# An expert weight's norm product two tiles later, and a reordered first down half, in a one-core attention and mixture-of-experts kernel

## The reference

```python
x = x + tanh(g_xattn) * xattn(layernorm(x), ctx, w_xattn)      # x: 16 x 128 x 1024
x = x + tanh(g_ffn) * ffn(layernorm(x), ...)

def xattn(feature, embedding, weight):   # three taps of the row, each weighted by a cosine of neighbours
    sim = stack([cos(emb, emb_left), cos(emb, emb), cos(emb, emb_right)])
    return einsum('bit,oi->bot', unfold3(feature) * repeat(sim, C), weight)

def ffn(h):
    rw = top2(h @ gate_w).sum(-1)
    shared = relu(h @ up_w) ** 2 @ down_w                  # 1024 -> 2048 -> 1024
    routed = ((h @ fc1_w) @ expert_w * rw) @ fc2_w         # 1024 -> 512 -> 512 -> 1024
    return layernorm(shared + routed, ln_gamma, ln_beta)
```

## Time and profile before

| what | value |
|---|---|
| median of 3 runs | 993.27 us |
| profiled execution | 992.8 us, span from first to last instruction 990.8 us |
| TensorE busy | 945.3 us, 95% of the span |
| VectorE, ScalarE, GpSimd busy | 491.2 us, 323.3 us, 319.0 us |
| mean granted TensorE clock | 0.985 of 2.4 GHz |
| TensorE's waits | 13.3 us (first weights), 10.6 us (L1309), 6.6 us (L1411), 2.7 us (L1357) |

### The profile page before, as it was taken

The page is one execution under the profiler, slowest core; times in us unless marked ns, Lnnn a source line. Parts: engine busy times, 40 slices in busy tenths (PEclk is TensorE's granted clock), DMA queues, the critical chain, the costliest instruction groups (busy, mean ns, idle before and its releaser), DMA issues.

```text
span 990.8 us, 12369 instructions
## 1 busy us (share of the span) xinstructions
PE 945.3 (95%) x4562; PEld 441.1 (45%) x4562; DVE 491.2 (50%) x859; ACT 323.3 (33%) x437; POOL 319.0 (32%) x147
## 2 busy tenths in 40 slices
PE   4989599799999999999999999999999999999995
PEld 2448244344444444444444444444444444444442
DVE  6677678985762345365662236355563222211112
ACT  3578775743331123242321122233332122211111
POOL 4220322238572431242572422142672200001110
PEclk9999799889999999999999999999999999999998
DMA  8796976343414543323414443422324233200001
GB/s 318 258 350 234 358 277 216 87 128 86 125 46 128 177 150 131 109 86 86 127 43 129 163 144 130 130 86 85 100 71 128 86 107 107 64 1 21 9 14 43
DMA packets 63359, 127.15 MB, mean 128 GB/s; under 512 B 35250, under 2 KB 35378, under 8 KB 62146
## 3 DMA queue, kind: packets, MB, share of 16 engines
q1 hardware_dynamic: 62290, 124.04, 38.2%
q10 hardware_dynamic: 1008, 2.30, 0.8%
HBM read 100.96 MB, written 19.07 MB: 121 GB/s over the span
## 4 chain that ended last, share of the span: by engine, by line
PE 85%; DVE 4%; ACT 3%; DMA 2%; issue 2%; DVEq 1%; ACTq 1%; SPq 1%; POOL 0%
PE psS L1411 32%; PE psS L1357 20%; PE psR L1357 20%; PE psR L1421 8%; PE psP L1320 5%; DMA big<-in_w_fc 1%; DVEq L906 1%; DMA xT<-in_ctx 1%; ACT hid L801 1%; DVE s L935 0%; ACT hid L812 0%; DVE ring L971 0%; DMA sim_scratch<-simo 0%; ACTq L811 0%; DVE s L939 0%
## 5 line engine op out<-in xcount | busy, mean ns | idle before, releaser
L1411 PE MATMUL psS<-big,hid 128*128 128x512 f16 x1536 | 337.4, 381 | 6.9 <-issue 6.6
L1411 PEld LDWEIGHTS psS<-big,hid 128*128 128x128 f16 x1536 | 150.4, 98 | 189.2 <-issue 9.4
L1357 PE MATMUL psS<-xT,ring 128*128 128x512 f16 (+1 forms) x912 | 191.5, 370 | 3.8 <-DVE xT L1060 2.7
L1357 PE MATMUL psR<-xT,ring 128*128 128x512 f16 (+1 forms) x912 | 190.2, 368 | 0.0
L1357 PEld LDWEIGHTS psS<-xT,ring 128*128 128x128 f16 x912 | 89.9, 99 | 102.5 <-DVE xT L1060 2.8
L1357 PEld LDWEIGHTS psR<-xT,ring 128*128 128x128 f16 x912 | 89.3, 98 | 97.1
L542 POOL TENSOR_TENSOR y<-y,lgb 128x1024 f32<-128x1024 f32 x15 | 39.2, 2612 | 252.8 <-ACT y L679 252.8
L1078 DVE SCALAR_TENSOR_TENSOR y<-psR,rw,y 128x1024 f32<-128x1024 f32 x15 | 19.2, 1281 | 141.0 <-PE psR L1421 141.0
L1421 PE MATMUL psR<-w,lgb 128*128 128x512 f16 x384 | 85.5, 379 | 0.0
L512 POOL TENSOR_TENSOR sides<-scr 128x1024 f32<-128x1024 f32 x12 | 30.1, 2506 | 141.7 <-DMA scr<-in_ctx 141.7
L532 POOL TENSOR_TENSOR ring<-f_buf,ring 128x1024 f32<-128x1024 f32 x18 | 39.2, 2177 | 99.7 <-ACT f_buf L647 60.4
(11 more groups left out here) (203 smaller groups left out, 989.1 us busy)
## 6 DMA issues: line engine op xcount, KB each, us to landing
ring<-pair_scratch SPq DMA_DIRECT2D x60, 512.0 KB, 3.3
ring<-sim_scratch SPq DMA_DIRECT2D x18, 504.0 KB
big<-in_w_up SPq DMA_DIRECT2D x8, 1024.0 KB, 6.4
out_rows<-y SPq DMA_DIRECT2D x15, 512.0 KB, 3.0
hid<-in_w_down SPq DMA_DIRECT2D x14, 512.0 KB, 6.1
big<-in_w_down SPq DMA_DIRECT2D x14, 512.0 KB, 6.9
pair_scratch<-ring SPq DMA_DIRECT2D x12, 512.0 KB, 6.9
scr<-in_ctx SPq DMA_DIRECT2D x9, 576.0 KB, 3.8
```

Source lines behind the costliest of these rows:

```text
L1357: mm = pe.matmul(up_bank[t % NR][:, cols], rows[:, a, k, :], xT[:, k, b, cols], start=(k == 0 and a == 0 and b == 0), stop=(k == KB - 1 an ...
L1411: mm = pe.matmul(psS[:, HALF * h:HALF * h + HALF], hT[:, i, a, P * j:P * j + P], dn[:, i, b, HALF * h:HALF * h + HALF], start=(i == 0 and ...
```

## The change

Five edits, all in the start-up stage and in block 0:

- `W2_SCALE_T` goes from 5 to 7: TensorE's small product for `w2` stands behind tile 6 instead of tile 4, and VectorE's reading of it at t = 7 instead of 5.
- The first row of down half 0: TensorE makes the whole shared product, then the routed one, then the attention of row (1, 0); before, that attention stood behind 12 of 16 slices.
- The same shared product waits for each slice of its input (`h_rdy`, i+1) and of the weights; before, it waited ahead of its first matmul for 14 of the 16 input slices and for `w2`. The wait for `w2` now stands ahead of the routed product.
- ScalarE and VectorE follow: the last three slices of the down matrix are split ahead of the rounding of row (1, 0) and of the routing, and the taking of row 0's result (`take_s`, `take_r`, `y_stats`, `finish`) comes ahead of `combine`. `take_s` now waits for `f_los` and `f_lo` of row (1, 0), as it writes a buffer that these read.
- In the start-up stage the turned halves of row 1 are taken out of PSUM earlier: on ScalarE ahead of `w2_evac(3)` and one square of the up matrix, on VectorE ahead of `combine(0, 2)`.

```diff
-        W2_SUM_T, W2_SCALE_T = 3, 5
+        W2_SUM_T, W2_SCALE_T = 3, 7
-        XATTN_AT, XATTN_FIRST = (5, 0, 0, 0), (12, 12, 10, 6)
+        XATTN_AT, XATTN_FIRST = (5, 0, 0, 0), (None, 12, 10, 6)
@@ ScalarE, end of up half 0
+                    for c in DN_LATE:
+                        dn_split_hi(c)
                 if phase_a:
                     f_his(m, 0)
@@ ScalarE, down half
                     if first and j == 0:
-                        for c in DN_LATE:
-                            dn_split_hi(c)
+                        act.wait_ge(f_lo_v, 2)
+                        act.wait_ge(f_lo_p, 1)
+                        take_s(n, j, phase_a)
                     if phase_a:
                         if j < BB - 1:
                             std(LX, BB * m + j + 1)
                             f_rows(m, j + 1)
+                        if first and j == 0:
+                            finish(n, j)
                         std(L1, BB * m + j)
                         x1_normal(m, j)
                         x_hi(m, j)
-                        if first and j == 0:
-                            take_s(n, j, phase_a)
                         if j < BB - 1:
                             f_his(m, j + 1)
@@ ScalarE, start-up
             up_square(0)
-            up_square(1)
-            w2_evac(3)
             first_xt_hi(1, 0)
             first_xt_hi(1, 1)
+            w2_evac(3)
+            up_square(1)
@@ VectorE, end of up half 0
+                if first:
+                    for c in DN_LATE:
+                        dn_lo(c)
+                    f_los(m, 0)
                 routing(n)
-                if phase_a:
+                if phase_a and not first:
                     f_los(m, 0)
@@ VectorE, down half
-                    if first and j == 0:
-                        for c in DN_LATE:
-                            dn_lo(c)
                     if phase_a:
                         if j < BB - 1:
                             x_stats(m, j + 1)
+                        if first and j == 0:
+                            take_r(n, j)
+                            y_stats(n, j)
                         combine(m, j)
                         x_lo(m, j)
@@ VectorE, start-up
-            combine(0, 2)
             first_xt_lo(1, 0)
             first_xt_lo(1, 1)
+            combine(0, 2)
             combine(0, 3)
@@ TensorE, shared()
                     if first:
+                        pe.wait_ge(h_rdy, i + 1)
                         pe.wait_ge(dn_rdy, i + 1)
@@ TensorE, down half
+                    if first and j == 0:
+                        pe.wait_ge(up_evac, UT - 2)
+                        shared(0, 0, IT, True).then_inc(s_done, 1)
+                        pe.wait_ge(up_evac, UT)
+                        pe.wait_ge(w2_rdy, LT)
+                        routed(0, 0, LT).then_inc(r_done, 1)
+                        xattn(m, 0)
+                        continue
                     if j == 0:
                         pe.wait_ge(up_evac, UT * (n + 1) - 2)
                         pe.wait_ge(h_rdy, IT * (n + 1) - 2)
-                        if first:
-                            pe.wait_ge(w2_rdy, LT)
```

More of the change, by code:

```diff
@@ L776, in down_half @@
                         take_s(n, j, phase_a)
-                    if phase_a or j < BB - 1:
-                        finish(n, j)
+                        if phase_a or j < BB - 1:
+                            finish(n, j)
                 if not phase_a:
@@ L1214, in down_half @@
                         continue
-                    take_r(n, j)
-                    y_stats(n, j)
+                    if not (first and j == 0):
+                        take_r(n, j)
+                        y_stats(n, j)
             def last_rows():
@@ L1440, in down_half @@
                         done = (XATTN_FIRST if first else XATTN_AT)[j]
-                        shared(j, 0, done, first and j == 0)
+                        shared(j, 0, done)
                         xattn(m, j)
                     if j == 0:
-                        shared(j, done, IT - 2, first)
+                        shared(j, done, IT - 2)
                         done = IT - 2
                         pe.wait_ge(h_rdy, IT * (n + 1))
-                    shared(j, done, IT, first and j == 0).then_inc(s_done, 1)
+                    shared(j, done, IT).then_inc(s_done, 1)
                     if j > 0:
```

## The result

The changed kernel takes **1003.5 us** (median of 4 runs, 1002.39 to 1006.71), the kernel before 992.7 us in the same comparison (four runs, 991.49 to 993.35). The ratio is 1.0119, 95% interval 1.0098 to 1.014: slower by 1.2% (the two medians lie 10.8 us apart), where 990.2 us had been forecast. The profiled execution took 1002.39 us with a span of 1000.6; the one before 992.8 with 990.8.

The account below looks back on a forecast made before the run. TensorE is busiest (945.3 of 990.8 us), but other engines keep most of its 24 us at stake. Up half 2.4 plus row 2's start 0.9 less loads 0.2 gives 3.1 us: median 990.2 us, range 984.5 to 994.5.

Parts of the forecast that it names:

- the start of row 2: First down half: psS free at 257.9 us instead of 260.98, 3.1 us gained, or 0.9 us after the slow clock.
- the 0.2 taken off for the loads: Row (1, 3): later cosine loads move `f_lo` to 296 or 297.5 us, close to TensorE's need at 297.65; 0.2 us lost.
- The up half, 2.4 us: Start-up and first up half: 1.1 us from the earlier turned halves and 1.3 us from the `w2` edit.
- the prediction's own sign ("or not at all"): Tile 19's relu at 197.5 us (before 199.94); forecast wrong if over 4 us earlier or not earlier at all.
- the give-back: Up half: `w2`'s scale takes 1.6 us of VectorE's lead; tile 8's lo half meets GpSimd, ending about 1.9 us late.
- this meeting: End of up half, 195.81 us: VectorE's lo half waited for GpSimd, taking 2.83 us instead of 0.68.
- The slow clock: Half clock on TensorE behind the 5.9 us stall ahead of row 2, costing 2.2 us.
- The rigid chain: GpSimd, first down half: `weigh` of row (1, 2) starts 16.0 us behind `f_lo` of row (1, 1).
- the first down half's start without a wait: First shared product: TensorE starts at 192.0 us, gaining the whole 6.62 us wait and the slow clock there.
- The small product behind tile 14: Up half, down matrix: a new TensorE wait of 5 to 8 us (there at 150.8, sum ready about 158), costing nothing.
- The slower one: Rival 3: row (1, 3)'s late cosine loads stop TensorE a second time, 995.4 us; chance 0.12.

Follow-up runs that it names:

- e5: The changed kernel with GpSimd finishing row (0, 0) ahead of `weigh` of row (1, 2): 996.85 us, ratio 1.0055 to the kernel before.
- e6: The changed kernel with both e4's spread additions and e5's earlier finish of row (0, 0) on GpSimd: 992.63 us, ratio 1.0021 to the kernel before.
- e11: The changed kernel with e9's order of GpSimd: 994.17 us, ratio 1.0026 to the kernel before.
- e3: The kernel before with the down half edits alone, without the `w2` and start-up edits: 1001.06 us, ratio 1.0106.
- e8: The kernel before with only the first shared product's waits changed (input rows one by one, `w2` ahead of the routed product): 991.64 us, ratio 1.0004.
- e9: e8 with GpSimd's first down half reordered: three additions later, rows (0, 0) and (0, 1) finished ahead of `weigh`: 990.29 us, ratio 0.999 to the kernel before.
- e10: e9 with the first attention behind 14 slices instead of 12 and `take_s` of row (0, 0) earlier: 987.93 us, ratio 0.9962 to the kernel before.
- e12: The kernel before with e9's order of GpSimd alone: 991.5 us, ratio 1.0003.
- e4: The changed kernel with GpSimd's additions of the first down half spread, three of four moved behind later rows' `f_lo`: 999.36 us, ratio 1.008 to the kernel before.
- e7: e6 with ScalarE's `take_s` of row (0, 1) ahead of the three roundings of row (1, 2): 997.0 us, ratio 1.0051 to the kernel before.
- e1: The kernel before with the `w2` edit alone (small product behind tile 6, read at t = 7): 990.87 us, ratio 0.9998.
- e2: The kernel before with the start-up edit alone (row 1's turned halves taken earlier): 992.24 us, ratio 1.0011.

## Why the prediction was wrong

The forecast was 990.2 us, the measured time 1003.5: outside the range, and on the other side.

- **The step that failed** is in the first down half: "ScalarE rounds the third row, 1.0 us, and only then comes `take_s` of row (0, 1), 1.1 us: psS is free at 257.9 us." GpSimd and the roundings came as reckoned on the clock of before, without the 2.4 us that were to come off: `f_lo` of row (1, 1) at 232.5 (233.2), `weigh` 16.1 us behind it at 248.55 (249.2), the third rounding done at 257.3 (256.8). But `take_s` waits also for the store of row (0, 0), which stands behind `weigh` and the finish on GpSimd: 265.6 + 1.1 = 266.7. In the prediction's sum the start of row 2 counted as 3.1 us gained, with 2.4 more from the up half; it was 5.8 us lost. e5, e6 and e11 show it: with the finish ahead of `weigh` the wait falls to 10.9, 6.0 and 6.9 us and the ratio from 1.0119 to 1.0055, 1.0021 and 1.0026, which is 6.3, 9.7 and 9.2 us.
- **The numbers for it were there.** The store of before went out 4.9 us behind the end of `weigh` (251.92 to 256.80) and landed 2.7 us later. Behind the forecast's own `weigh`, done at 255.8, that is an estimate of 263.4 us for the landing and 264.5 for psS, 3.5 us after today's start and not 3.1 before. The other 2.2 us are GpSimd's longer instructions, less its start of 0.7 us ahead of the forecast.
- **The sum.** The forecast span was 987.7 us, the measured one 1000.6. The 12.9 us between them are 11.3 at the start of row 2 (5.8 lost, 5.5 forecast as gained), 0.3 of slow clock, 1.5 at the loop's second pass, which the forecast had at nothing, less the 0.2 taken off for the loads.
- The prediction read `take_s`'s releaser from the rows of before, where two came together and only the rounding shows. The code has the second in the line above the copy (`act.wait_ge(out_done, ...)`). It follows GpSimd's list to `weigh` and to the later loads; the finish of row (0, 0), which frees `y`, is not in it.
- **The up half, 2.4 us**, did not come. The relu of tile 19 was to start at 197.5 us and started at 200.60, 0.7 later than the 199.94 of before: by the prediction's own sign ("or not at all") it was wrong here too. Nor is there a gain in the other traces. With the old order that relu lies between 197.0 and 199.9 us in six traces (the kernel before, e3, e8, e9, e10, e12), with both edits between 199.2 and 202.0 in six (the changed kernel, e4 to e7, e11). e1 and e2 each bring nothing that can be measured. The first part of the give-back was as described: tile 8's lo half took 2.84 us (so in the changed kernel, e4, e7 and e11; in e1, e5 and e6 it took 0.7, so the meeting is indeed decided by tenths). Then a second meeting came at the end of the half. VectorE's timeline of the changed kernel:

```profile
133.88 2.84 DVE L1184 TENSOR_TENSOR hid<-sim_side,hid 128x512 f16<-128x512 f32 x1
...
190.60 5.95 DVE L1112 SCALAR_TENSOR_TENSOR big<-big,wsc 128x1024 f16<-128x1024 f32 x2 [0.22 <-ACT big L753]
196.47 2.83 DVE L1184 TENSOR_TENSOR hid<-sim_side,hid 128x512 f16<-128x512 f32 x1
...
205.23 0.69 DVE L1184 TENSOR_TENSOR hid<-sim_side,hid 128x512 f16<-128x512 f32 x1
```

  Two slices of the down matrix took 5.95 us instead of 4.2, as GpSimd's `weigh` came a little earlier against them. They started 1.1 us ahead of before (190.60 against 191.67), and the last lo half, at 205.23 against 205.74, has 0.5 us left of that. The prediction has this meeting move as a whole.
- **The slow clock**, 2.2 us reckoned, cost 2.5; right in kind and size. **The rigid chain** `f_lo` to `weigh` (16.0 against 16.1 us) and the first down half's start without a wait were right. The small product behind tile 14 waited 2.0 us, not the 7 reckoned, since TensorE had been held for 5.0 us ahead of tile 13 already. Ahead of none of the relus of tiles 5 to 19 did ScalarE wait for TensorE, so neither costs anything.
- **The rivals.** The slower one had the wrong place: the loads of row (1, 3) gave TensorE no second stop (`f_lo` at 294.03 us, its attention at 306.85). That GpSimd's chain decides was right, which of its ends was not.

## What to carry to other kernels

Where two releasers free an instruction at the same moment, a profile names only one of them; when one is to move, read every semaphore ahead of the instruction in the code, and follow each back to the engine whose list it hangs on. A single output buffer ties a row's start to the store of the row before it, through every engine that finishes that row: before moving work ahead of it, look at what the finishing engine has queued in front. And removing a wait of the busiest engine is worth nothing while another chain sets the pace: the order of the helpers has to be changed in the same step. Here that is shown in the traces, where row 2 starts at 257.45 us in e8 and 254.67 in e9, and only weakly in the time: e8 and e12 gave nothing, the two together (e9) 0.1%, and e10, with two more moves, 0.4%.

## What the runs showed of the hardware

- Behind the 14.6 us stall the clock stood at 0.50 for 17.1 us, longer than the 10.2 us behind the stalls of before, but what of it fell on work was the same: the stretch ended 5.1 us after TensorE had taken up work, against 4.5 and 4.6 us, and it cost 2.5 us against 2.0 and 2.4. In the variants, stalls of 6.0 to 13.0 us ahead of row 2 cost 2.0 to 2.8 us in the same way (60 matmuls in 15.14 us in e4, 15.96 in e11, against 13.12): the price does not follow the length of the stall.
- Idle of 3.2 us ahead of row 3's transposes left the clock at full speed in the changed kernel, where the 2.68 us idle of before had been followed by a stretch at 0.50 to 0.61 that ended 3.9 us later. The stop of 2.0 to 2.5 us at the loop's second pass was followed by half clock in e7 to e10 (46 matmuls in 11.55 to 11.78 us) and by full speed in the changed kernel, e3 to e6 and e11 (10.09 us).
- VectorE and GpSimd stood in each other's way for longer than one instruction: at 190.60 us two VectorE instructions of 1.28 us each took 5.95 us together while GpSimd ran a row of three, of which the second and third took 3.34 and 3.33 us instead of 2.35.
